# Moving the wide work of a step behind the wait for the maxima, in a single-core attention and feed-forward kernel

## The chip, the cores and the metric

The kernel runs on one core of one Trainium2 chip. The metric is device time in microseconds. Of the kernel before there are three runs: 6168.65, 6160.35 and 6164.67 us, median 6164.67. The engines are called PE (TensorE, matrix products, with PEld for its weight loads), DVE (VectorE), ACT (ScalarE), POOL (GpSimd) and SP (SyncE, which here issues the DMAs). PE's granted clock over the profiled execution was 0.986 of full speed.

## The reference

One layer of attention with relative positions, then a feed-forward layer with a router, each between layer norms and with a residual:

```python
def attn(x, ...):                      # x: (16, 1024, 256), 16 heads of 16
    q, k, v = (split_heads(lin(x, W, b)) for W, b in ((Wq, bq), (Wk, bk), (Wv, bv)))
    rel = rel_emb[r[None, :] - r[:, None] + 511]
    qk = einsum('bhld,bhrd->bhlr', q, k) / 4 + einsum('bhld,lrd->bhlr', q, rel)
    out = einsum('bhlr,bhrd->bhld', softmax(qk, axis=-1), v)
    return lin(merge_heads(out), Wo, bo)

def ffn(x, ...):                       # 6 experts of rank 16, the best 2 are used
    h = einsum('bsi,eri->bser', x, routed_A)
    routed = einsum('bseo,bse->bso', einsum('bser,eor->bseo', h, routed_B), sparse_w)
    return x @ base_W.T + base_b + (x @ shared_A.T) @ shared_B.T + routed

x = x + layernorm(attn(layernorm(x)))
x = x + layernorm(ffn(layernorm(x)))
```

## The kernel before

The 16 x 1024 rows are cut into 128 tiles t of 128 rows of queries. A tile is worked in 16 steps g = 0 to 15: `jp = g // 4` is the quarter of the keys (256 of them, in two blocks c = 0, 1), `k = g % 4` the block of 32 queries, of all 16 heads at once. The tiles overlap: while tile t goes through its scores, PE also makes the projections of a later tile n (`proj`), finishes the attention of the tile before (`a`) and does the feed-forward layer of the one before that (`b`). Tiles 2 to 127 have all parts and are the main loop, unrolled six times.

Each engine has its own queue, whose order is the order in which the code is written; semaphores tie the queues together. A step g on PE is, before the change:

1. `scores(g, 0)`: 8 matmuls (line 681) and 12 (line 687) into one PSUM bank of `sc`.
2. `transpose_max` (line 695): turns the row maxima `r1`, which DVE found in the scores of step g-1, into `p_max` in the PSUM bank `pm`.
3. `scores(g, 1)`: another 20 matmuls, then the signal `s_scores`.
4. `wide`: work into the PSUM bank `pw`. With k = 1 and k = 2 it is a half of the value product (`pv`, line 714), with k = 3 the transposition of the result (`transpose_parts`, line 721), with k = 0 and jp < 3 a projection of tile n (line 726 in step 0, line 735 in steps 4 and 8).
5. `mixed`: work into the bank `pm`, where DVE still reads `p_max`: a transposed row of `nm` with k = 1 (line 754), and in steps 0, 3, 8, 10, 11 and 12 transpositions and products of the `a` and `b` parts. Ahead of each stands `maxima_read`, the wait for `s_nmr`.
6. `shift` (line 704): 16 matmuls that subtract the maxima from the scores of step g-1, with `nmm` as weights. It waits for `s_nm`.

DVE does in each step: `spread` of g-1, that is `nm` (line 1000, a reduce that reads `p_max`, signal `s_nmr`) and then `nmm` (line 1003, a multiply, signal `s_nm`); the maximum of the scores of step g (line 991, called `r` in the profile); and `side`, small operations of the other parts. In step 5 `side` holds the router's `gate` (line 1034), `ceq` (line 1039) and `cgt` (line 1040), in step 6 three more operations on these, in step 14 the statistics of `x1` and `y2n`, in step 15 `xn1`. ACT copies what PE leaves in `pw` and `pm` (line 868) and takes the exponential of the shifted scores (line 876); it waits for each in the order of its own queue, in step 3 for `hf`, then `parts`, then the exponential. The scores have three buffers. POOL splits numbers into two halves of 16 bits and does additions; its chain `wp`, `osum`, `qkb`, `qkh`, `qkl` (lines 599 to 568) begins when ACT has copied the last `parts` of a tile, in step 3.

Of the kernel before, what the change touches and what calls it, by code (L numbers as in the profile page):

```python
# [20 lines left out]
NG = NJP * NI  # L21
# [17 lines left out]
def buffer(t, g):  # L39


    return (t * NG + g) % NBUF


def sandwich_kernel(nc, x, wqT, bq, wkT, bk, wvT, bv, woT, bo, relT, baseT, base_b,
# [13 lines left out]
    with ctx:  # L59
# [3 lines left out]
        def sem(name):  # L63
            return ctx.enter_context(nc.semaphore(name))
# [200 lines left out]
        s_nmr = sem("s_nmr")  # L265
# [13 lines left out]
        def batch_of(t):  # L279
            return t // TPB  # L280
# [387 lines left out]
        def _(pe):  # L668
# [39 lines left out]
            def pv(jp, half):  # L708

                for col in (2 * half, 2 * half + 1):  # L710
                    for c in range(2):
                        for q in range(4):
                            h = 4 * col + q
                            last = mm(pw[32 * q:32 * q + 32, col * P:(col + 1) * P], vs[:, 2 * jp + c, h, :],  # L714
                                      prob[:, jp % 2, c, h, :], start=(c == 0), stop=(c == 1))
                return last

            def transpose_parts(stage):
                pe.wait_ge(s_ot, stage + 1)
                for col in range(4):  # L720
                    last = nc.tensor.transpose(pw[:, col * P:(col + 1) * P], ot[:, col, :], ident[:, :])  # L721
                last.then_inc(s_ott, 1)

            def transpose2(dst, src):
                for c in range(2):
                    last = nc.tensor.transpose(dst[:, c * P:(c + 1) * P], src[:, c * P:(c + 1) * P],
                                               ident[:, :])
                return last

            def product(dst, *pairs):  # L730


                steps = [(lhs(i), rhs(j)) for lhs, rhs in pairs for i, j in ((0, 0), (0, 1), (1, 0))]
                for m, (lhs, rhs) in enumerate(steps):
                    last = mm(dst, lhs, rhs, start=(m == 0), stop=(m == len(steps) - 1))  # L735
                return last

            def both(lhs, rhs, cols=slice(None)):

                return [(lambda i, c=c: lhs[:, i, c, cols], lambda j, c=c: rhs[:, j, c, :]) for c in range(2)]  # L740

            def maxima_read(t, g, old):

                if old:
                    pe.wait_ge(s_nmr, t * NG + g)

            def mixed(t, g, att, a, b):


                jp, k = divmod(g, NI)  # L750
                old = a if g == 0 else att
                if k == 1 and (a if jp == 0 else att):
                    maxima_read(t, g, old)
                    mm(p_n[:, 0:H], nm[:, (jp - 1) % 2, :], ident16[:, 0:H], start=True, stop=True)\  # L754
                        .then_inc(s_nmtp, 1)
                    return s_nmt, t * NJP + jp
                if g == 0 and b:
                    maxima_read(t, g, old)
                    pe.wait_ge(s_xn1, t - 1)
                    transpose2(p_t, xn1).then_inc(s_x1Tp, 1)  # L760
                    return s_x1T, t - 1
                if g == 3 and b:

                    maxima_read(t, g, old)
                    pe.wait_ge(s_x1T2, t - 1)
                    product(p_t[:, 0:NH], *both(x1T2, w_a2)).then_inc(s_hp, 1)
                    return s_hf, t - 1
                if g == 8 and a:
                    maxima_read(t, g, old)
                    pe.wait_ge(s_o, t)  # L770
                    transpose2(p_t, o[:, :, :].rearrange("p h d -> p (h d)")).then_inc(s_oTp, 1)
                    return s_oT, t
                if g == 11 and a:
                    maxima_read(t, g, old)
                    pe.wait_ge(s_oT2, t)
                    product(p_t, *both(oT2, w_o2)).then_inc(s_wo, 1)
                    return s_y0, t
                if g == 10 and b:
                    maxima_read(t, g, old)
                    pe.wait_ge(s_hw, t - 1)  # L780
                    nc.tensor.transpose(p_n[0:NA, :], hw[:, :], ident[:, :]).then_inc(s_hTp, 1)
                    return s_hT, t - 1
                if g == 12 and b:
                    maxima_read(t, g, old)
                    pe.wait_ge(s_hT2, t - 1)
                    product(p_t, *both(x1T2, w_base2), (lambda i: hT2[:, i, :], lambda j: w_b2[:, j, :]))\
                        .then_inc(s_y2p, 1)
                    return s_y20, t - 1
                return None

            def wide(t, n, g, att, proj, a):

                jp, k = divmod(g, NI)
                if k and (a if jp == 0 else att):
                    pj = (jp - 1) % NJP
                    if k == 1:
                        pe.wait_ge(s_exp, t * NG + g - 1)
                        pe.wait_ge(s_vs[pj], batch_of(t - 1 if jp == 0 else t) * 16 + 16)

                        if proj and jp < 3:  # L800
                            pe.wait_ge((s_xT, s_qkf, s_vf)[jp], n + 1)
                        else:
                            pe.wait_ge(s_part, t * NJP + jp - 1)
                        pv(pj, 0)
                    elif k == 2:
                        pv(pj, 1).then_inc(s_pv, 1)
                    else:
                        transpose_parts(t * NJP + jp - 1)
                if k == 0 and jp < 3 and proj:

                    if a if jp == 0 else att:
                        pe.wait_ge(s_part, t * NJP + jp - 1)
                    elif jp == 0:
                        pe.wait_ge(s_vf, n)
                    if jp == 0:
                        pe.wait_ge(s_xn, n + 1)
                        transpose2(pw[:, 0:2 * P], xn).then_inc(s_xTp, 1)
                    elif jp == 1:
                        pe.wait_ge(s_xT2, n + 1)
                        for m, w in enumerate((w_q2, w_k2)):  # L820
                            for e in range(2):
                                last = product(pw[:, (2 * m + e) * P:(2 * m + e + 1) * P],
                                               *both(w, xT2, slice(e * P, (e + 1) * P)))
                        last.then_inc(s_qkp, 1)
                    else:
                        pe.wait_ge(s_qkf, n + 1)
                        product(pw[:, 0:D], *both(xT2, w_v2)).then_inc(s_vp, 1)

            def tile(t, n, att, proj, a, b, ph=None):
                read = None  # L830
                for g in range(NG):
                    jp, k = divmod(g, NI)
                    old = a if g == 0 else att
                    if att:
                        if k == 0:
                            pe.wait_ge(s_tw[jp], t * 16 + 16)
                            pe.wait_ge(s_ks[jp], batch_of(t) * 96 + 96)
                        if g == 0:
                            pe.wait_ge(s_qm, t * 96 + 96)
                        if jp == 0:  # L840
                            pe.wait_ge(s_mask, t * NI + k + 1)
                        free = t * NG + g - NBUF + 1
                        if not (isinstance(free, int) and free <= 0):
                            pe.wait_ge(s_exp, free)
                        scores(g, 0, buffer(ph, g), ph % 2)
                    if read is not None:
                        pe.wait_ge(*read)
                    if old:
                        transpose_max(t * NG + g)
                    if att:  # L850
                        scores(g, 1, buffer(ph, g), ph % 2).then_inc(s_scores, 1)

                    wide(t, n, g, att, proj, a)
                    read = mixed(t, g, att, a, b)
                    if old:
                        shift(buffer(ph, g - 1), t * NG + g)

            passes(pe, tile)


# [277 lines left out]
```

## Time and profile before

| what | value |
|---|---|
| runs | 6168.65, 6160.35, 6164.67 us |
| profiled execution | 6168.65 us |
| its span, first to last instruction | 6166.9 us |
| PE busy | 5870.1 us, 161792 matmuls |
| DVE busy | 4998.3 us, 81% |
| POOL, ACT busy | 3349.6 us (54%), 3069.7 us (50%) |
| DMA | 589.60 MB, mean 96 GB/s |

The busy share of an engine is an average; what the engine waits for is read from the list of waits and from the timeline, where instructions of one line that follow each other are merged into one row (so 32 records of line 714 are one row of 1.08 us). The start of a row is when the first of them began. Matmuls overlap in the pipeline, so a row of PE can begin before the one ahead of it has ended. All rows of timelines below are of one tile of the main loop, near the middle of the execution: step 2 begins near 2987.5 us, step 6 near 2998.8, step 12 near 3016.5.

### The profile page before, as it was taken

What the parts mean: (1) busy time and instruction counts of PE and PEld (TensorE: products, weight loads), DVE (VectorE), ACT (ScalarE), POOL (GpSimd) and SP (SyncE); (2) the same over time, 40 slices, a digit from 0 to 9 for tenths busy, and PEclk for the clock granted to TensorE, in tenths of its full rate; (3) what the DMA queues carried; (4) which work ended last, traced back from release to release, by engine and by line L of the source; (5) the groups of instructions that cost most, each with busy time, mean ns of one, the idle gap of its engine ahead of it and who ended that gap; (6) DMA issues with size and microseconds to landing.
All of it is one profiled execution on the core that took longest, in us unless ns stands there. A gap on an engine that the chain in (4) does not pass through costs nothing.

```text
span 6166.9 us, 379525 instructions
## 1 busy us (share of the span) xinstructions
PE 5870.1 (95%) x161792; PEld 5396.8 (88%) x161792; DVE 4998.3 (81%) x10289; ACT 3069.7 (50%) x5145; POOL 3349.6 (54%) x5226
## 2 busy tenths in 40 slices
PE   3999999999999999999999999999999999999997
PEld 2998988889898888988898988888898989898896
DVE  2788888888888888888888888888888878888886
ACT  1555555555455555545555555555555545555553
POOL 4455555555555555555555555555555555555555
PEclk7999999999999999999999999999999999999998
DMA  4334343343433334343343433434333343433432
GB/s 109 94 83 108 93 107 89 90 108 87 108 92 98 95 90 107 87 106 94 83 112 91 105 88 92 106 86 112 89 98 96 93 103 84 108 95 84 114 89 51
DMA packets 1461396, 589.60 MB, mean 96 GB/s; under 512 B 1127504, under 2 KB 1425472, under 8 KB 1459696
## 3 DMA queue, kind: packets, MB, share of 16 engines
q1 hardware_dynamic: 1459696, 565.02, 36.4%
q8 instruction: 1301, 21.32, 1.5%
q14 instruction: 399, 3.27, 0.2%
HBM read 476.43 MB, written 89.78 MB: 92 GB/s over the span
## 4 chain that ended last, share of the span: by engine, by line
PE 72%; DVE 14%; issue 6%; DVEq 5%; POOLq 1%; ACT 1%; POOL 1%; SPq 0%; DMA 0%
PE sc L687 18%; PE pw L714 13%; PE sc L704 13%; PE sc L681 12%; DVE r L991 6%; PE pm L735 4%; PE pw L735 4%; DVEq L1002 4%; PE pm L695 4%; PE pw L721 2%; DVE nmm L1003 2%; DVE xn L957 2%; DVE nm L1000 1%; DVE gate L1034 1%; DVE y2n L957 1%
## 5 line engine op out<-in xcount | busy, mean ns | idle before, releaser
L991 DVE TRANSPOSE_TENSOR_REDUCE r<-sc 128x32 f16<-128x1024 f32 x2048 | 2543.9, 1242 | 46.0 <-PE sc L687 45.1
L876 ACT ACTIVATE prob<-sc 128x1024 f32<-128x1024 f32 x2048 | 2097.9, 1024 | 294.4 <-PE sc L704 265.6
L687 PE MATMUL sc<-rm,tw 128*128 128x48 f16 (+1 forms) x49152 | 2148.5, 195 | 7.8 <-issue 7.3
L687 PEld LDWEIGHTS sc<-rm,tw 128*128 128x128 f16 x49152 | 1757.2, 100 | 9.5 <-issue 8.7
L681 PE MATMUL sc<-qm,ks 96*128 96x64 f16 x32768 | 1639.6, 193 | 52.5 <-DMA ks<-qk_s 28.3
L704 PE MATMUL sc<-nmm,pick 128*128 128x64 f16 x32768 | 1299.0, 193 | 95.6 <-DVE nmm L1003 84.5
L704 PEld LDWEIGHTS sc<-nmm,pick 128*128 128x128 f16 x32768 | 1128.1, 98 | 264.9 <-DVE nmm L1003 193.5
L681 PEld LDWEIGHTS sc<-qm,ks 96*128 96x128 f16 x32768 | 1300.4, 98 | 67.9 <-issue 50.4
L1000 DVE TENSOR_REDUCE nm<-pm 16x32 f16<-16x256 f32 x2048 | 836.3, 408 | 562.8 <-PE pm L695 549.4
L714 PE MATMUL pw<-prob,vs 128*32 128x128 f32 x32768 | 1114.3, 276 | 13.0 <-issue 4.3
L553 POOL TENSOR_TENSOR rm<-raw,mask_r 128x192 f16<-128x192 f16 (+1 forms) x1545 | 886.1, 602 | 34.6 <-DMA raw<-qk_s 23.2
L714 PEld LDWEIGHTS pw<-prob,vs 128*32 128x32 f32 x32768 | 840.4, 110 | 73.7 <-issue 17.5
L1003 DVE TENSOR_TENSOR nmm<-nm,mask_h 16x64 f16<-16x64 f16 x2048 | 590.1, 288 | 204.6 <-issue 19.4
L695 PE MATMUL pm<-ident,r 128*128 128x128 f16 x4096 | 571.7, 221 | 0.9 <-DVE r L991 0.8
L566 POOL TENSOR_TENSOR oT<-oT,one 128x256 f16<-128x256 f32 x128 | 78.4, 612 | 866.9 <-ACT oT L868 866.9
L868 ACT ACTIVATE ot<-pw 128x512 f32<-128x512 f32 x512 | 304.9, 595 | 486.3 <-PE pw L714 486.3
L868 ACT ACTIVATE nmt<-pm 128x16 f32<-128x16 f32 x512 | 93.7, 183 | 766.3 <-PE pm L754 766.3
L599 POOL TENSOR_TENSOR wp<-parts,wst 128x1088 f32<-128x1088 f32 x128 | 262.4, 2050 | 184.7 <-ACT parts L868 184.7
L560 POOL TENSOR_TENSOR ve<-mv,eps 128x1 f32<-128x1 f32 x521 | 113.6, 218 | 411.7 <-DVE mv L954 411.5
L562 POOL TENSOR_TENSOR rs<-ve,mhalf 128x1 f32<-128x1 f32 x521 | 288.2, 553 | 76.4 <-issue 2.5
L721 PE MATMUL pw<-ident,ot 128*128 128x128 f32 x2048 | 325.0, 281 | 0.7 <-ACT ot L868 0.7
L566 POOL TENSOR_TENSOR hT<-hT,one 112x128 f16<-112x128 f32 x128 | 51.1, 399 | 487.2 <-ACT hT L868 487.2
(129 smaller groups left out, 5958.9 us busy)
## 6 DMA issues: line engine op xcount, KB each, us to landing
raw<-qk_s SPq DMA_DIRECT2D x3096, 64.0 KB, 2.7
tw<-tw_s SPq DMA_DIRECT2D x512, 288.0 KB, 3.6
v_s<-vpad SPq DMA_DIRECT2D x136, 256.0 KB, 3.4
vs<-v_s SPq DMA_DIRECT2D x64, 512.0 KB, 4.4
qm<-qk_s SPq DMA_DIRECT2D x774, 32.0 KB, 2.1
ks<-qk_s SPq DMA_DIRECT2D x384, 64.0 KB, 3.3
xin<-x SPq DMA_DIRECT2D x138, 128.0 KB, 3.4
qk_s<-qkh SPq DMA_DIRECT2D x272, 64.0 KB, 2.9
```

The costliest lines, as they stand in the source:

```text
L553: last = g.tensor_tensor(rm[:, i, :, c * H:(c + n) * H].rearrange("p m (h e) -> p m h e", e=n), src[:, :, :, q:q + n], mask_r[:, c:c + n]. ...
L681: last = mm(bank[:, 2 * h * IW:(2 * h + 2) * IW], ks[:, h, j:j + P], qm[:, qb, 2 * h:2 * h + 2, i * IW:(i + 1) * IW], start=(h == 0), stop ...
L687: last = mm(out3[:, :, OCT * m + q:OCT * m + q + n], tw[:, s, jp, u:u + P], rm[:, i, m, r * H:(r + n) * H].rearrange("p (h e) -> p h e", e=n),
L695: last = mm(p_max[:, c * P:(c + 1) * P], r1[:, c * H:c * H + P], ident16[:, :], start=True, stop=True)
L704: last = mm(pairs[:, :, h, :], pick[:, h, :], nmm[:, :, :], start=False, stop=True, skip_group_check=True)
L714: last = mm(pw[32 * q:32 * q + 32, col * P:(col + 1) * P], vs[:, 2 * jp + c, h, :], prob[:, jp % 2, c, h, :], start=(c == 0), stop=(c == 1))
L721: last = nc.tensor.transpose(pw[:, col * P:(col + 1) * P], ot[:, col, :], ident[:, :])
L735: last = mm(dst, lhs, rhs, start=(m == 0), stop=(m == len(steps) - 1))
L876: A(prob[:, jp % 2, :, :, i * IW:(i + 1) * IW], sc[:, 2 * buf:2 * buf + 2, :].rearrange("p c (h i) -> p c h i", i=IW), ACT.Exp).then_inc(s ...
L991: v.tensor_reduce(r1[:, 0:2 * H], sc[:, 2 * buf:2 * buf + 2, :].rearrange("p c (h i) -> p (c h) i", i=IW), axis=AX.X, op=ALU.max, apply_tr ...
L1000: v.tensor_reduce(part, p_max[0:H, :].rearrange("h (q i) -> h i q", i=IW), axis=AX.X, op=ALU.max, negate=True).then_inc(s_nmr, 1)
L1003: v.tensor_tensor(nmm[0:H, :, :], part.rearrange("h (a i) -> h a i", a=1) .to_broadcast((H, 2, IW)), mask_h[:, :, :], ALU.mult).then_inc(s ...
```

## The change

On PE alone, `maxima_read` is gone. Each step that has a shift now waits for `s_nmr` once, directly ahead of `mixed`, also in the steps where `mixed` does nothing. `wide` stays ahead of this wait where k = 1 and in steps 0 and 8; in all others it comes behind it and behind `mixed`.

```diff
-            def maxima_read(t, g, old):
-
-                if old:
-                    pe.wait_ge(s_nmr, t * NG + g)
-
             def mixed(t, g, att, a, b):
 
 
                 jp, k = divmod(g, NI)
-                old = a if g == 0 else att
                 if k == 1 and (a if jp == 0 else att):
-                    maxima_read(t, g, old)
+
                     mm(p_n[:, 0:H], nm[:, (jp - 1) % 2, :], ident16[:, 0:H], start=True, stop=True)\
                         .then_inc(s_nmtp, 1)
                     return s_nmt, t * NJP + jp
                 if g == 0 and b:
-                    maxima_read(t, g, old)
                     pe.wait_ge(s_xn1, t - 1)
...
@@ -850,8 +838,14 @@
                     if att:
                         scores(g, 1, buffer(ph, g), ph % 2).then_inc(s_scores, 1)
 
-                    wide(t, n, g, att, proj, a)
+                    wide_first = k == 1 or g in (0, 8)
+                    if wide_first:
+                        wide(t, n, g, att, proj, a)
+                    if old:
+                        pe.wait_ge(s_nmr, t * NG + g)
                     read = mixed(t, g, att, a, b)
+                    if not wide_first:
+                        wide(t, n, g, att, proj, a)
                     if old:
                         shift(buffer(ph, g - 1), t * NG + g)
```

PE's queue in step 6, from the last score matmul to the next step's first ones, before:

```order
L687 MATMUL sc<-rm,tw 128x16x3
L714 MATMUL pw<-prob,vs 32x128 x16
L704 MATMUL sc<-nmm,pick 128x2x32 [waits s_nm]
L704 MATMUL sc<-nmm,pick 128x2x32 x15
L681 MATMUL sc<-qm,ks 128x64 [waits s_exp]
L681 MATMUL sc<-qm,ks 128x64 x7
```

and after the change:

```order
L687 MATMUL sc<-rm,tw 128x16x3
L714 MATMUL pw<-prob,vs 32x128 [waits s_nmr]
L714 MATMUL pw<-prob,vs 32x128 x15
L704 MATMUL sc<-nmm,pick 128x2x32 [waits s_nm]
L704 MATMUL sc<-nmm,pick 128x2x32 x15
L681 MATMUL sc<-qm,ks 128x64 [waits s_exp]
L681 MATMUL sc<-qm,ks 128x64 x7
```

The value product (line 714) now carries the wait for `s_nmr`, and the shift (line 704) stands behind it as before. Steps 2 and 14 are the same, step 7 has line 721 and step 4 line 735 in its place.

PE's queue in step 3, where `mixed` is the product of `x1T2` and `w_a2` (line 735) and `wide` the transposition of `ot` (line 721), before:

```order
L687 MATMUL sc<-rm,tw 128x16x3
L721 MATMUL pw<-ident,ot 128x128 [waits s_ot]
L721 MATMUL pw<-ident,ot 128x128 x3
L735 MATMUL pm<-w_a,x1T 128x118 [waits s_x1T2,s_nmr]
L735 MATMUL pm<-w_a,x1T 128x118 x5
L704 MATMUL sc<-nmm,pick 128x2x32 [waits s_nm]
L704 MATMUL sc<-nmm,pick 128x2x32 x15
```

and after:

```order
L687 MATMUL sc<-rm,tw 128x16x3
L735 MATMUL pm<-w_a,x1T 128x118 [waits s_x1T2,s_nmr]
L735 MATMUL pm<-w_a,x1T 128x118 x5
L721 MATMUL pw<-ident,ot 128x128 [waits s_ot]
L721 MATMUL pw<-ident,ot 128x128 x3
L704 MATMUL sc<-nmm,pick 128x2x32 [waits s_nm]
L704 MATMUL sc<-nmm,pick 128x2x32 x15
```

The two have changed places, and the wait for `s_nmr` is now ahead of both. Step 11 is alike, with `w_o2` and `oT2`.

PE's queue in step 10, where `mixed` is the transposition of `hw` (line 781 before, 770 after), before:

```order
L687 MATMUL sc<-rm,tw 128x16x3
L714 MATMUL pw<-prob,vs 32x128 x16
L781 MATMUL pm<-ident,hw 112x128 [waits s_hw,s_nmr]
L704 MATMUL sc<-nmm,pick 128x2x32 [waits s_nm]
L704 MATMUL sc<-nmm,pick 128x2x32 x15
```

and after:

```order
L687 MATMUL sc<-rm,tw 128x16x3
L770 MATMUL pm<-ident,hw 112x128 [waits s_hw,s_nmr]
L714 MATMUL pw<-prob,vs 32x128 x16
L704 MATMUL sc<-nmm,pick 128x2x32 [waits s_nm]
L704 MATMUL sc<-nmm,pick 128x2x32 x15
```

The transposition and its two waits went ahead of the value product. No matmul was added or removed, and the queues of DVE, ACT, POOL and SP are the same in both kernels.

## Rows read from the trace of the kernel before

**Rows 1.** Busy time of the engines, and the page's chain that ended last, by engine.

```profile
PE 5870.1 (95%) x161792; PEld 5396.8 (88%) x161792; DVE 4998.3 (81%) x10289; ACT 3069.7 (50%) x5145; POOL 3349.6 (54%) x5226
...
PE 72%; DVE 14%; issue 6%; DVEq 5%; POOLq 1%; ACT 1%; POOL 1%; SPq 0%; DMA 0%
```

**Rows 2.** List of waits: engine, line, waited for; us in total, times, longest us.

```profile
DVE nm L1000 <- PE pm L695: 549.4, 926, 4.4
...
PE sc L704 <- DVE nmm L1003: 84.5, 234, 1.1
```

**Rows 3.** Timeline of PE, steps 6 and 7: start us, us, engine, line.

```profile
3000.14 1.08 PE L714 MATMUL pw<-prob,vs 128*32 128x128 f32 x32
3001.72 0.64 PE L704 MATMUL sc<-nmm,pick 128*128 128x64 f16 x16 [0.51 <-DVE nmm L1003]
...
3003.27 0.52 PE L687 MATMUL sc<-rm,tw 128*128 128x48 f16 x12
3003.62 0.63 PE L721 MATMUL pw<-ident,ot 128*128 128x128 f32 x4
3004.33 0.64 PE L704 MATMUL sc<-nmm,pick 128*128 128x64 f16 x16
```

**Rows 4.** Timeline of DVE, steps 5 to 7.

```profile
2999.20 0.53 DVE L1034 TENSOR_SCALAR gate<-eg,rg 128x6 f32<-128x6 f32 x1
...
2999.91 1.15 DVE L1040 TENSOR_TENSOR cgt<-gate 128x36 f32<-128x36 f32 x1
3000.99 0.41 DVE L1000 TENSOR_REDUCE nm<-pm 16x32 f16<-16x256 f32 x1
...
3003.60 0.40 DVE L1000 TENSOR_REDUCE nm<-pm 16x32 f16<-16x256 f32 x1
```

**Rows 5.** Groups by form, DVE: count, busy us, mean ns of one, idle before.

```profile
L1040 DVE TENSOR_TENSOR cgt<-gate 128x36 f32<-128x36 f32 x128 | 147.4, 1151 | 0.0
...
L1043 DVE TENSOR_TENSOR ceqt<-ceq,tri 128x36 f32<-128x36 f32 x128 | 25.1, 196 | 11.8
```

**Rows 6.** Timeline of all engines, step 12.

```profile
3017.43 0.41 DVE L1000 TENSOR_REDUCE nm<-pm 16x32 f16<-16x256 f32 x1 [1.03 <-PE pm L695]
...
3017.46 0.52 PE L687 MATMUL sc<-rm,tw 128*128 128x48 f16 x12
...
3017.90 0.83 PE L735 MATMUL pm<-w_base,x1T 128*128 128x256 f16 x6
```

**Rows 7.** Timeline of PE, steps 2 and 3.

```profile
2988.15 0.52 PE L687 MATMUL sc<-rm,tw 128*128 128x48 f16 x12
2988.60 1.08 PE L714 MATMUL pw<-prob,vs 128*32 128x128 f32 x32
2989.61 0.64 PE L704 MATMUL sc<-nmm,pick 128*128 128x64 f16 x16
...
2991.03 0.52 PE L687 MATMUL sc<-rm,tw 128*128 128x48 f16 x12
2991.39 0.63 PE L721 MATMUL pw<-ident,ot 128*128 128x128 f32 x4
2991.86 0.48 PE L735 MATMUL pm<-w_a,x1T 128*128 128x118 f16 x6
```

**Rows 8.** Timeline of POOL, steps 5 and 6.

```profile
2998.66 1.04 POOL L566 TENSOR_TENSOR qkh<-qkb,one 128x512 f16<-128x512 f32 x1 [0.20 <-issue]
2999.84 1.17 POOL L568 TENSOR_TENSOR qkl<-qkb,qkh 128x512 f16<-128x512 f32 x1
```

**Rows 9.** Timeline of all engines, step 10.

```profile
3011.95 0.41 DVE L1000 TENSOR_REDUCE nm<-pm 16x32 f16<-16x256 f32 x1
...
3012.00 1.08 PE L714 MATMUL pw<-prob,vs 128*32 128x128 f32 x32
```

**Rows 10.** Timeline of all engines, step 15.

```profile
3026.22 0.41 DVE L1000 TENSOR_REDUCE nm<-pm 16x32 f16<-16x256 f32 x1
...
3026.45 0.64 PE L721 MATMUL pw<-ident,ot 128*128 128x128 f32 x4
```

More of the change, by code:

```diff
@@ L762, in mixed @@
                 if g == 3 and b:
-                    maxima_read(t, g, old)
                     pe.wait_ge(s_x1T2, t - 1)
@@ L768, in mixed @@
                 if g == 8 and a:
-                    maxima_read(t, g, old)
                     pe.wait_ge(s_o, t)
@@ L773, in mixed @@
                 if g == 11 and a:
-                    maxima_read(t, g, old)
                     pe.wait_ge(s_oT2, t)
@@ L778, in mixed @@
                 if g == 10 and b:
-                    maxima_read(t, g, old)
                     pe.wait_ge(s_hw, t - 1)
@@ L783, in mixed @@
                 if g == 12 and b:
-                    maxima_read(t, g, old)
                     pe.wait_ge(s_hT2, t - 1)
```

## The prediction

> **What bounds the kernel now.** Three views, from coarse to fine. The page's busy times and its chain of waits come first: PE is busy 95% of the span and holds 72% of the chain that ended last, DVE 81% and 14% [rows 1]. So PE sets the pace, and what is to be found is where PE stands still. The list of waits answers that: of PE's waits inside the main loop, the largest is the shift (line 704) waiting for `nmm` from line 1003, 84.5 us in 234 places [rows 2]. The third view is the timeline of one tile, read step by step: one tile is 16 steps g = 0 to 15, and tiles t = 2 to 127, 126 of them, run all parts. I read the tile that begins near 2983 us.
>
> In step 6 PE starts the second half of the value product at 3000.14, 32 records that last 1.08 us, and then stands 0.51 us before the shift at 3001.72 [rows 3]. DVE is the reason: its `cgt` lasts 1.15 us, so `nm` starts only at 3000.99 and ends at 3001.40, and `nmm` follows it [rows 4]. 126 x 0.51 = 64 us, three quarters of the 84.5 us. That this repeats in each tile is in the table by form: `cgt` has a mean of 1151 ns over 128, a sister of the same shape (`ceqt`) one of 196 ns [rows 5].
>
> **What the change does to one step.** PE's queue is in order. A step ends with the shift, which needs `nmm`, made from `nm`. Before, "wide" work (value product, transposition of its result, projections) stands ahead of the wait for `nm` and so covers DVE's reduce as well as its multiply. After, in steps 2, 3, 4, 6, 7, 10, 11, 14 and 15, the wait for `nm` (semaphore s_nmr) stands in front of the wide work, which covers only the multiply. No matmul is added or removed. In one step alone the new order can never be earlier: wide work starts at the later of two moments where it started at the first alone. The price of a step is the end of `nm`, plus the signal, less the moment at which PE was free, and PE is given back whatever it had waited for `nmm` afterwards. The signal is measured where the wait already stands directly behind the scores, in step 12: `nm` ends at 3017.84, the product starts at 3017.90, so 0.06 us; the last score matmuls started at 3017.46, so a step that DVE follows at once starts its next work 0.44 after them [rows 6]. Queued behind each new wait is all later PE work, with ACT's exponential and DVE's next maximum behind that.
>
> Steps 3, 4 and 11 (unhindered, `nm` follows PE). In step 3 line 721 starts at 2991.39, 0.36 after the scores' last group at 2991.03 [rows 7]; steps 4 and 11 show the same distance. With 0.44 in place of 0.36 each loses 0.08. The order of lines 721 and 735 turns round in 3 and 11, with the same matmuls; I take 0 for it. The turned pair is not in the trace; the old one follows at 0.47 [rows 7], and it could hardly gain or lose more than a third of that, 0.16. Step 4's two projections still hide `nmm` as before. Sum 3 x 0.08 = 0.24.
>
> Steps 2 and 14: the value product starts 0.45 after the scores' last group (2988.60 against 2988.15 [rows 7]), later than the 0.44 of the signal. Cost 0; bounds 0 and 0.1 each.
>
> Step 6: the wait ends at 3001.40 + 0.06 = 3001.46, where the product started at 3000.14 before. Product to shift, unhindered, takes 1.01 (2988.60 to 2989.61 [rows 7]). The shift moves to 3002.47 from 3001.72: +0.75. `nm` here does not depend on the new waits but on `cgt`, which ends at 3001.06, 0.05 after POOL's `qkl` at 3001.01 [rows 4, 8]. That POOL chain begins with `wp`, behind ACT's copy of `parts` in step 3, which the turned order puts a little later; 0.05 more. Bounds 0.55 (POOL's chain keeps its old time while PE comes 0.24 later) and 1.0. I take 0.80.
>
> Step 7: before, line 721 started at 3003.62 and the shift at 3004.33, 1.06 after the scores' last group (3003.27), held by the `nmm` behind an `nm` that ends at 3004.00 [rows 3, 4]. DVE was late because of its three operations after `cgt`. PE now comes 0.8 later and DVE only as much later as its own operations require, so `nm` again follows PE: start at 0.44, plus 0.47 for the transposes, shift at 0.91 instead of 1.06. This gives back 0.15. Steps 8 and 9 keep their order and cost nothing.
>
> Step 10: the transpose of `hw` goes ahead of the value product. `nm` ended at 3012.36 where PE was ready at 3012.00 [rows 9], but PE is then 0.7 later and most of this is gone; the pause between product and next load moves rather than vanishes. 0.05, bounds -0.1 and 0.42.
>
> Step 15: `nm` ends at 3026.63, signal 3026.69, against 3026.45 for line 721 [rows 10]: 0.24. Step 0 behind it waits for DVE's `xn` anyway, and PE's lateness is absorbed there; I take 0.05, bounds 0 and 0.24.
>
> **Sum.** Per tile 0.24 + 0 + 0.80 - 0.15 + 0.05 + 0.05 = 0.99 us; times 126 = 125 us. The profiled execution took 6168.65 us (span 6166.9), so 6293; it is 4.0 us above the median of the three runs, so 6289, or 6290 rounded. Nothing outside these steps changes: ACT gets `hf`, `hT` and `y0` earlier, but PE's next wait for them lies behind a full round of scores and shows no loss in the list before.
>
> **The rivals.**
> *Lateness adds up.* If DVE comes later by as much as PE does, every step pays its full distance: 0.24, then 1.32, 0.44 (3004.00 + 0.06 against 3003.62), 0.42 and 0.24 for steps 6, 7, 10 and 15, less the 0.51 already stood: 2.15 per tile, 271 us, 6436 on the median. For it: DVE's maximum follows `nmm`. Against: in step 7 DVE had been the later one, and `nm` waited for PE for 549.4 us in 926 places [rows 2].
> *DVE sets the pace and takes the delay up.* If what step 6 loses (0.65 with step 7) is regained before the tile ends, 0.34 stays: 43 us, 6208. For it: DVE's 81% share. Against: those same 926 places, where DVE idles for PE.
> *Faster: POOL slips out of `cgt`'s way.* `gate` starts at 2999.20 inside POOL's `qkh` (2998.66 to 2999.70) and `cgt` ends with `qkl` [rows 4, 8]. If POOL's chain came over 0.54 later against DVE, `gate` and `cgt` would run first, some 0.3 and 0.95 shorter. `nm` would then follow PE, and step 6 loses its wait of 0.51, step 7 its 0.15 and step 8 a few hundredths: -0.70, with +0.24, +0.10 and 0.05 at most for the rest, so -0.3 per tile, -39 us, 6126. Against: the chain's start moves by some 0.1, PE's and so DVE's by about as much. The point from which it decides is 0.54 us.
> The Trainium skill, SBUF, "Who interferes with whom", says that a VectorE instruction with two SBUF inputs and a GpSimd instruction that reads SBUF exclude each other, and that the one issued first goes first; by that rule the slip would indeed free `cgt`. Here the trace agrees as to the block (1151 against 196 ns), and no row shows the reverse order.
>
> **How the numbers follow.** Forecast 0.78, adding up 0.08, taken up 0.09 (its lower end, 0.02, within 0.2%), POOL slips 0.05. A change under 0.2%, 12 us, can't be told from none here. So faster 0.05, same 0.02, slower 0.93. The forecast's own ends: 0.70 per tile (step 6 at 0.55, the rest as taken) gives 6253; 1.5 per tile (steps 2 and 14 at 0.1, step 6 at 1.0, 10 and 15 at 0.15 each) 6350. The range goes a little into both neighbours: 6245 to 6365.
>
> **What would show it.** In the profile after: PE's line 714 waiting on `nm` (line 1000) in 126 places with about 1.3 us each; the list's wait of the shift on `nmm` shrunk from 84.5 to some 20 us; `cgt` still near 1.15 us; line 721 of step 7 about 0.44 behind its scores; a tile's length up by 1 us. Wrong would be: `cgt` near 0.2 us; idle of line 721 of over 0.2 us in each tile (adding up); or line 695 waiting less than before by as much as line 714 waits more.

## The result, and the profile after

The changed kernel took 6230.68 us (median of 4 runs, 6229.27 to 6231.38), the kernel before, with its runs on the same chip, 6163.78 us. The ratio is 1.011, with a 95% interval of 1.0098 to 1.0124: slower by 67 us, where 125 had been forecast, and below the range's lower end of 6245. The profiled execution took 6235.45 us, its span is 6233.7.

The page of the changed kernel, its row of busy times and its chain by engine, against [rows 1]:

```profile
PE 5857.5 (94%) x161792; PEld 5428.1 (87%) x161792; DVE 4998.5 (80%) x10289; ACT 3139.6 (50%) x5145; POOL 3362.3 (54%) x5226
...
PE 73%; DVE 13%; issue 6%; DVEq 6%; POOLq 1%; ACT 1%; POOL 0%; SPq 0%; DMA 0%
```

PE has the same 161792 matmuls and is busy 12.6 us less in a span that is 66.8 us longer. So the added time is idle time of PE. Its list of waits (us in total, times, longest us), against [rows 2]:

```profile
DVE nm L994 <- PE pm L695: 581.2, 1045, 2.0
...
PE pw L714 <- DVE nm L994: 132.8, 126, 1.1
...
PE sc L704 <- DVE nmm L997: 22.4, 103, 0.3
```

The wait of the shift on `nmm` fell from 84.5 to 22.4 us, as forecast. The new one, of the value product on `nm`, is there 126 times, 1.05 us each on PE. Together that is 70.7 us more. Steps 6 and 7 of one tile, on PE, against [rows 3]. The rows of line 695 are where `transpose_max` begins; from here on a step's length is the distance from its row of line 695 to the next one:

```profile
3079.83 0.28 PE L695 MATMUL pm<-ident,r 128*128 128x128 f16 x2
...
3080.18 0.52 PE L687 MATMUL sc<-rm,tw 128*128 128x48 f16 x12
3081.71 1.08 PE L714 MATMUL pw<-prob,vs 128*32 128x128 f32 x32 [1.02 <-DVE nm L994]
3082.73 0.64 PE L704 MATMUL sc<-nmm,pick 128*128 128x64 f16 x16
...
3083.44 0.52 PE L687 MATMUL sc<-rm,tw 128*128 128x48 f16 x12
3083.80 0.28 PE L695 MATMUL pm<-ident,r 128*128 128x128 f16 x2
...
3084.14 0.52 PE L687 MATMUL sc<-rm,tw 128*128 128x48 f16 x12
3084.58 0.66 PE L721 MATMUL pw<-ident,ot 128*128 128x128 f32 x4
3085.07 0.63 PE L704 MATMUL sc<-nmm,pick 128*128 128x64 f16 x16
...
3086.13 0.28 PE L695 MATMUL pm<-ident,r 128*128 128x128 f16 x2
```

Before, the value product of step 6 started 0.46 after the scores' last group and the shift waited; now the product starts at 3081.71, 1.53 after the scores' last group, and the shift 1.02 behind it. Step 6 is 3.97 us long and step 7 only 2.33. DVE in the same stretch, against [rows 4]:

```profile
3080.18 1.15 DVE L1034 TENSOR_TENSOR cgt<-gate 128x36 f32<-128x36 f32 x1
3081.26 0.41 DVE L994 TENSOR_REDUCE nm<-pm 16x32 f16<-16x256 f32 x1
...
3081.87 1.25 DVE L985 TRANSPOSE_TENSOR_REDUCE r<-sc 128x32 f16<-128x1024 f32 x1
...
3084.11 0.41 DVE L994 TENSOR_REDUCE nm<-pm 16x32 f16<-16x256 f32 x1 [0.16 <-PE pm L695]
```

`nm` of step 6 ends at 3081.67, and 0.04 later the product starts: the signal is as short as assumed. The rows of the kernel before that I had not read are those of line 695, of the same tile as [rows 3]:

```profile
2999.34 0.28 PE L695 MATMUL pm<-ident,r 128*128 128x128 f16 x2
...
3002.43 0.52 PE L687 MATMUL sc<-rm,tw 128*128 128x48 f16 x12
3002.91 0.28 PE L695 MATMUL pm<-ident,r 128*128 128x128 f16 x2
...
3005.51 0.28 PE L695 MATMUL pm<-ident,r 128*128 128x128 f16 x2
```

and the row of DVE's maximum that belongs to it:

```profile
3001.60 1.25 DVE L991 TRANSPOSE_TENSOR_REDUCE r<-sc 128x32 f16<-128x1024 f32 x1
```

In the changed kernel line 695 begins 0.36 after the group of line 687 ahead of it (3083.44 to 3083.80). In the kernel before it is 0.48 (3002.43 to 3002.91): the maximum ended at 3002.85, and line 695 started 0.06 later. So PE waited for DVE a second time at the end of step 6, by 0.12, and again at the end of steps 7 and 8: as means over 122 tiles line 695 came 0.14, 0.13 and 0.12 later than it does where DVE is ready. The list of waits does not name these waits; they are short, and PE's earlier matmuls still count as busy. In the kernel before, these two steps were 3.57 and 2.60 us long.

The two kernels step by step, as means of the distance between the first weight loads of line 695, over 122 tiles of the main loop of each trace (changed minus before, us per tile):

| step | measured | forecast | what it is |
|---|---|---|---|
| 3 | +0.05 | +0.08 | wait for `nm`, turned order |
| 4 | +0.13 | +0.08 | wait for `nm`, and in a few tiles a late `nm` (last section) |
| 6 | +0.43 | +0.80 | wait for `nm` ahead of the value product |
| 7 | -0.27 | -0.15 | DVE no longer late |
| 8 | -0.08 | 0 | the same |
| 10 | +0.20 | +0.05 | turned order, and a late `nm` in a third of the tiles |
| 11 | -0.01 | +0.08 | turned order |
| 15 and 0 | +0.07 | +0.05 | wait for `nm`, then `xn` |
| the rest | -0.01 | 0 | |
| sum | +0.52 | +0.99 | times 126: 65 us and 125 us |

### The profile page after: what moved, and what is told of

The parts are those of the page before. It is cut to its first block, busy times and chain, and to the rows that moved or that the text cites. A ratio compares the mean times of both kernels' runs of the same rounds, so it can differ in the third digit from the quotient of the medians.

```text
span 6233.7 us, 379790 instructions
## 1 busy us (share of the span) xinstructions
PE 5857.5 (94%) x161792; PEld 5428.1 (87%) x161792; DVE 4998.5 (80%) x10289; ACT 3139.6 (50%) x5145; POOL 3362.3 (54%) x5226
## 4 chain that ended last, share of the span: by engine, by line
PE 73%; DVE 13%; issue 6%; DVEq 6%; POOLq 1%; ACT 1%; POOL 0%; SPq 0%; DMA 0%
PE sc L687 18%; PE pw L714 14%; PE sc L704 13%; PE sc L681 12%; DVE r L985 5%; PE pm L735 5%; DVEq L996 4%; PE pw L735 4%; PE pm L695 3%; PE pw L721 3%; DVE xn L951 2%; DVE nm L994 1%; DVE nmm L997 1%; DVE y2n L951 1%; PE pm L748 1%
## 5 line engine op out<-in xcount | busy, mean ns | idle before, releaser
L704 PE MATMUL sc<-nmm,pick 128*128 128x64 f16 x32768 | 1299.1, 193 | 28.9 <-DVE nmm L997 22.4
L704 PEld LDWEIGHTS sc<-nmm,pick 128*128 128x128 f16 x32768 | 1146.1, 98 | 167.9 <-issue 104.5
L553 POOL TENSOR_TENSOR rm<-raw,mask_r 128x192 f16<-128x192 f16 (+1 forms) x1545 | 886.7, 603 | 33.9 <-DMA raw<-qk_s 22.4
L862 ACT ACTIVATE parts<-pw 128x272 f32<-128x272 f32 x512 | 203.5, 398 | 268.8 <-PE pw L721 262.1
```

The lines of the kernel that those rows point to most:

```text
L553: last = g.tensor_tensor(rm[:, i, :, c * H:(c + n) * H].rearrange("p m (h e) -> p m h e", e=n), src[:, :, :, q:q + n], mask_r[:, c:c + n]. ...
L704: last = mm(pairs[:, :, h, :], pick[:, h, :], nmm[:, :, :], start=False, stop=True, skip_group_check=True)
L862: return A(dst, src, ACT.Copy)
```

## The experiments

All kernels were timed in turn with the kernel before on their chip; a ratio is to that. Where I give a change in us it is the difference of the medians. Step lengths of experiments are means over 16 or 17 tiles in the middle of each trace, or over 122 tiles of the main loop where that is said.

### Step 6 alone

```diff
+                    if old and g == 6:
+                        pe.wait_ge(s_nmr, t * NG + g)
                     wide(t, n, g, att, proj, a)
                     read = mixed(t, g, att, a, b)
```

> The kernel before with one new wait: in step 6 alone PE waits for nm ahead of the value product. Theory A (DVE paces steps 6 to 8 and takes most of the delay up: behind nm of step 6 its maximum, its side work and the next nm follow without a gap, and PE waits for the maximum at line 695): from nm of step 6 to line 695 of step 9 the kernel before takes 7.26 us and the changed one 7.57, so +0.31 per tile, 39 us, about 6203. Theory B (PE paces, as I had predicted): +0.75 - 0.15 = 0.60 per tile, 76 us, about 6240.

Measured: 6190.40 us against 6161.44, ratio 1.0038 (1.0025 to 1.0052), +29 us. PE of steps 6 and 7:

```profile
3010.67 0.28 PE L695 MATMUL pm<-ident,r 128*128 128x128 f16 x2
...
3012.71 1.08 PE L714 MATMUL pw<-prob,vs 128*32 128x128 f32 x32 [1.18 <-DVE nm L1002]
...
3014.79 0.28 PE L695 MATMUL pm<-ident,r 128*128 128x128 f16 x2
...
3017.03 0.29 PE L695 MATMUL pm<-ident,r 128*128 128x128 f16 x2
```

Step 6 is 4.12 us (mean +0.58), step 7 only 2.24 (mean -0.34), together +0.24 per tile or 30 us. The shift moves by 0.73 (mean of 122 tiles), as I had thought; the step is longer by less than that, and more than half of it comes back in the next. Theory B (76 us) falls; theory A (39) was 10 us too high.

### All but step 6

```diff
-                    wide_first = k == 1 or g in (0, 8)
+                    wide_first = k == 1 or g in (0, 6, 8)
```

> The changed kernel with step 6 as before. Theory A: steps 6 to 8 lose only 0.09 per tile in the changed kernel, and without the wait step 6 would even be 0.17 shorter than before (POOL's chain comes earlier against PE), so 0.26 less per tile than the changed kernel: about 6198. Theory B: 0.65 less per tile, 82 us, about 6149.

Measured: 6198.88 us, ratio 1.0057 (1.0043 to 1.0070), +37 us, as theory A said. Step 6 alone (29) and all but step 6 (37) add up to 66, against 67 for the whole change. Step 6, whose code is here that of the kernel before, is 0.20 shorter than in it (122 tiles).

### Step 10 alone

```diff
-                    wide(t, n, g, att, proj, a)
+                    if g != 10:
+                        wide(t, n, g, att, proj, a)
                     read = mixed(t, g, att, a, b)
+                    if g == 10:
+                        wide(t, n, g, att, proj, a)
```

> The kernel before with the order of step 10 alone turned (transpose of hw with its waits, then the second half of the value product). Theory A (a switch between a product of 32 columns and other work costs a pause on each side, and the transpose no longer hides it): +0.20 per tile, 25 us, about 6189. As predicted (the pause only moves): +0.05 per tile, 6 us, about 6170.

Measured: 6180.78 us, ratio 1.0029 (1.0019 to 1.0040), +19 us; step 10 is 0.17 longer. The turned order in the changed kernel, PE of step 10, against [rows 9]:

```profile
3092.04 0.52 PE L687 MATMUL sc<-rm,tw 128*128 128x48 f16 x12
3092.47 0.32 PE L770 MATMUL pm<-ident,hw 128*112 128x128 f32 x1
3092.72 1.08 PE L714 MATMUL pw<-prob,vs 128*32 128x128 f32 x32
3093.74 0.64 PE L704 MATMUL sc<-nmm,pick 128*128 128x64 f16 x16
```

In this tile the transposition starts 0.43 after the scores' last group, where it waits for `nm`, the product 0.25 behind it and the shift 1.02 behind the product: 1.70 in all. In the old order it was 0.45 to the product, 1.01 to the transposition and 0.16 to the shift, 1.62. The product stands 0.25 behind the transposition where the shift stood 0.16 behind it, and the pause ahead of a product that follows the scores (0.45, where line 721 has 0.36) is no longer there to cover the wait. So turning the pair saves nothing and costs 0.08.

The rest of the 0.20 is in other tiles. Over 122 tiles of the changed kernel the shift moves by 0.08 in the 82 in which `nm` ends on time, and by 0.36 in the 40 in which it ends late (0.66 on average behind the scores' last group, in place of 0.38). The late ones are the last two of each six tiles of the unrolled loop, in which step 10 is 0.28 and 0.52 longer, and the tile that the prediction read is the last of its six. In such a last tile DVE pauses in step 9, in the kernel before as in the changed one:

```profile
3009.46 0.51 DVE L1003 TENSOR_TENSOR nmm<-nm,mask_h 16x64 f16<-16x64 f16 x1 [0.47 <-issue]
```

The profile names no releaser for this pause, and its cause stays open.

### `cgt` moved on DVE

```diff
                 if g == 5 and b:
...
                     v.tensor_tensor(ceq[:, :, :], gf, ge, ALU.is_equal)
-                    v.tensor_tensor(cgt[:, :, :], gf, ge, ALU.is_gt)
                 if g == 6 and b:
+                    v.tensor_tensor(cgt[:, :, :], gf, ge, ALU.is_gt)
                     dve.drain()
```

(`gf` and `ge` are formed again in step 6.) First on the kernel before:

> The kernel before with DVE's cgt moved from the end of step 5's side work to the start of step 6's, where POOL has ended qkl. Theory A (cgt was long only because it stood behind POOL's qkl; PE loses 0.51 us visibly and some 0.14 more at line 695 through it): cgt near 0.2 us, about -0.65 per tile, 82 us, about 6082. Theory C (only the visible wait goes): -0.51 per tile, about 6100. Theory D (POOL blocks it at the new place too, or DVE's total length sets steps 6 to 8): within 15 us of 6164.

Measured: 6090.81 us, ratio 0.9881 (0.9866 to 0.9896), 71 us faster than the kernel before, and so the fastest of all these kernels. It lies between theories A (6082) and C (6100): the shift of step 6 comes 0.53 earlier, and 0.08 more comes back at line 695, where A had 0.14. Theory D falls. The group of `cgt` (count, busy us, mean ns):

```profile
L1043 DVE TENSOR_TENSOR cgt<-gate 128x36 f32<-128x36 f32 x128 | 19.3, 151 | 0.0
```

It takes 151 ns in place of 1151 [rows 5]. Step 6 is 0.63 shorter, step 7 0.06 longer. Then the same move on the changed kernel:

> The changed kernel with DVE's cgt moved to the start of step 6's side work, to be compared with the kernel before with the same move (6091 us). Theory A (DVE is late in steps 6 to 8 whatever PE does): nm of step 6 then ends 0.63 after the scores' last loads, so its new wait costs about 0.2 and step 7 gives 0.1 back; with steps 3, 4, 10, 15 unchanged at +0.35: about +0.45 per tile, 57 us, 6148. Theory B (the wait in step 6 costs what nm is late there, nothing is given back): the 0.60 of my prediction falls to 0.2, so about +0.6 per tile in all, 76 us, 6167.

Measured: 6138.05 us, ratio 0.9964 (0.9951 to 0.9978), 47 us over the kernel before with the same move. That one ran on another chip; each against the kernel before on its own chip, it is 50 us (20 gained in place of 71). The change costs less where DVE is less late, but it still costs, in steps 3, 4 and 10. Theory A was 10 us too high, B 29.

### Step 7 alone

```diff
+                    if old and g == 7:
+                        pe.wait_ge(s_nmr, t * NG + g)
                     wide(t, n, g, att, proj, a)
```

> The kernel before with one new wait, in step 7 alone, ahead of line 721. PE comes to line 721 some 0.45 us later in each tile. Theory A: the shift moves by about 0.1 only, and PE then waits 0.14 less for DVE's maximum at line 695: 0 per tile, within 6 us of 6161. Theory E (lateness adds up): 0.44 per tile, 55 us, 6217. Theory F (only the shift's own move counts): 0.11 per tile, 14 us, 6175.

Measured: 6163.35 us against 6158.31, ratio 1.0008 (1.0000 to 1.0017), +5 us. Line 721 starts 0.43 later in each tile, step 7 is 0.08 longer, and step 8 is 0.08 shorter. A wait of 0.43 us on the busiest engine costs nearly nothing here: the sharpest blow to "lateness adds up".

### Who takes the delay up

If it is DVE's own lateness behind `nm` of step 6 that takes PE's delay up, taking that lateness away must make the wait dear. The base moves DVE's router work out of steps 6 and 7:

```diff
                     v.tensor_tensor(lg[:, :], hf[:, NA:NH], b_rt[:, :], ALU.add)
+                    v.tensor_copy(hw[:, 0:R], hf[:, 0:R])
...
-                if g == 6 and b:
-                    dve.drain()
-                    v.tensor_tensor(ceqt[:, :, :], ceq[:, :, :], tri[:, :, :], ALU.mult)
-                    dve.drain()
-                    v.tensor_tensor(cadd[:, :, :], cgt[:, :, :], ceqt[:, :, :], ALU.add)
-                    dve.drain()
-                    v.tensor_reduce(rank[:, :], cadd[:, :, :], axis=AX.X, op=ALU.add)
...
-                if g == 7 and b:
-
+                if g == 8 and b:
+                    dve.drain()
+                    v.tensor_tensor(ceqt[:, :, :], ceq[:, :, :], tri[:, :, :], ALU.mult)
+                    dve.drain()
+                    v.tensor_tensor(cadd[:, :, :], cgt[:, :, :], ceqt[:, :, :], ALU.add)
+                    dve.drain()
+                    v.tensor_reduce(rank[:, :], cadd[:, :, :], axis=AX.X, op=ALU.add)
                     dve.drain()
                     v.scalar_tensor_tensor(out=sw[:, :], in0=rank[:, :], scalar=2.0, in1=gate[:, :],
                                            op0=ALU.is_lt, op1=ALU.mult)
-                    v.tensor_copy(hw[:, 0:R], hf[:, 0:R])
-                if g == 8 and b:
```

> The kernel before with DVE's router work moved away from steps 6 and 7: ceqt, cadd, rank and sw to step 8's side work, the copy of hf to step 4's. The cgt that is blocked stays in step 5, so nm of step 6 is as late as before. It serves as the base of the next kernel. Theory A (DVE paces steps 6 to 8): step 7 gets shorter by 0.34 and step 8 by up to 0.2, step 9 or 10 gives some of it back: about -0.25 per tile, 6130. If DVE does not pace them: 6161.

Measured: 6177.02 us (11 runs, 6166.73 to 6191.67) against 6158.31, ratio 1.0031 (1.0022 to 1.0040): 19 us slower, where both theories had it faster or equal. The steps say why: step 7 is 0.35 and step 8 0.12 shorter, as theory A says, but step 9 is 0.59 longer, since `nm` there now comes behind six small operations of step 8. PE, steps 6 and 7:

```profile
3046.51 0.28 PE L695 MATMUL pm<-ident,r 128*128 128x128 f16 x2
...
3050.01 0.29 PE L695 MATMUL pm<-ident,r 128*128 128x128 f16 x2
...
3052.26 0.29 PE L695 MATMUL pm<-ident,r 128*128 128x128 f16 x2
```

As a base it does what it should: step 7 is at 2.25, PE's own length. On it, the wait of step 6:

> The kernel relieved of DVE's router work in steps 6 and 7, with the one new wait of step 6. Theory A: with DVE no longer late behind nm of step 6, nothing takes the delay up, and the wait costs about 0.6 us per tile, 76 us over its base, against 29 us over the kernel before. Theory G (the delay is given back by PE itself, since line 721 behind a wait is faster): the same 29 us over its base.

Measured: 6245.79 us against 6158.31, ratio 1.0138 (1.0122 to 1.0155). That is 69 us over its base, and its fastest run (6240.40) is still 49 us over the slowest of the base. PE and DVE of steps 6 and 7:

```profile
3033.95 0.28 PE L695 MATMUL pm<-ident,r 128*128 128x128 f16 x2
...
3036.06 1.08 PE L714 MATMUL pw<-prob,vs 128*32 128x128 f32 x32 [1.24 <-DVE nm L1002]
...
3038.14 0.28 PE L695 MATMUL pm<-ident,r 128*128 128x128 f16 x2
...
3040.39 0.28 PE L695 MATMUL pm<-ident,r 128*128 128x128 f16 x2
```

```profile
3036.22 1.25 DVE L993 TRANSPOSE_TENSOR_REDUCE r<-sc 128x32 f16<-128x1024 f32 x1
3038.46 0.41 DVE L1002 TENSOR_REDUCE nm<-pm 16x32 f16<-16x256 f32 x1 [0.99 <-PE pm L695]
```

Step 6 is 4.19 us where the base has 3.50 (means: 0.61 more), and step 7 stays at 2.25. DVE has ended its maximum at 3037.47 and waits for PE until 3038.46. The same wait, in the same step, costs 69 us here and 29 us where DVE is late behind it. Theory G falls, since line 721 stands behind a delayed shift in both.

### Step 3 alone, and a further move on DVE

```diff
-                    wide(t, n, g, att, proj, a)
+                    if g != 3:
+                        wide(t, n, g, att, proj, a)
+                    elif old:
+                        pe.wait_ge(s_nmr, t * NG + g)
                     read = mixed(t, g, att, a, b)
+                    if g == 3:
+                        wide(t, n, g, att, proj, a)
```

> The kernel before with step 3 alone changed: wait for nm, product of line 735, then line 721. As predicted: +0.08 per tile, 10 us, 6168. From the traces since: ACT's copy of parts, and with it POOL's chain, starts 0.11 us earlier in the tile, which lets cgt and nm of step 6 end up to 0.17 earlier against PE; step 3 itself +0.05, step 4 +0.01 (or +1.4 us in the few tiles where DVE's xn falls behind POOL's wp): together -0.1 to 0 per tile, 6146 to 6160.

Measured: 6173.00 us (12 runs, 6157.88 to 6188.10) against 6165.93, ratio 1.0010 (1.0000 to 1.0020). The +10 us of the first expectation lie within the interval, the second (12 us faster to equal) only touches its end. The trace shows what the second had too small. Over 122 tiles step 3 is at +0.10, step 4 at +0.13 and step 6 at -0.14. In 110 of the tiles step 3 loses 0.10 and step 6 gains 0.08, and little else moves. In the other 12 DVE's `xn` falls behind POOL's `wp` (last section): step 4 is 1.32 longer, step 6 0.70 and step 7 0.34 shorter.

The last run adds two moves on DVE to that of `cgt`:

```diff
                     v.tensor_tensor(lg[:, :], hf[:, NA:NH], b_rt[:, :], ALU.add)
+                    v.tensor_copy(hw[:, 0:R], hf[:, 0:R])
...
-                if g == 7 and b:
+                if g == 8 and b:
 
                     dve.drain()
                     v.scalar_tensor_tensor(out=sw[:, :], in0=rank[:, :], scalar=2.0, in1=gate[:, :],
                                            op0=ALU.is_lt, op1=ALU.mult)
-                    v.tensor_copy(hw[:, 0:R], hf[:, 0:R])
-                if g == 8 and b:
-
                     dve.drain()
```

> The kernel before with cgt in step 6 (as in the fourth run, 6091 us), the copy of hf into hw moved from step 7 to step 4 and sw from step 7 to step 8, both ahead of steps in which a value product covers DVE. If DVE paces step 8: nm of step 8 ends 0.25 earlier, step 8 is 0.1 shorter, 12 us, 6079. If moved work costs as much at the new places: 6091.

Measured: 6108.49 us against 6165.93, ratio 0.9907 (0.9893 to 0.9921), where the move of `cgt` alone had 0.9881. Step 8 is 0.11 shorter as expected, and step 9 is 0.15 longer. So the move of `cgt` alone stays the best version, though the ends of the two intervals touch.

## Why the prediction was wrong

The direction was right, and so was how the new wait delays PE: no step can gain by it alone, and step 6 is where `nm` is late. What was wrong is how much of the delay PE is given back. The sum was nearly twice too large, 0.99 us per tile against 0.52, and the steps that failed are these. (Numbers without a source are means over 122 tiles.)

**Step 6, "+0.75", then "0.80".** The 0.75 was right: with step 6 alone the shift moves by 0.73. What I left out stands at the end of the step. Before, PE lost another 0.14 at line 695, waiting for DVE's maximum, and this is given back as well: the step is 0.59 longer, not 0.73. And the 0.05 for POOL's chain had the wrong sign. With line 735 ahead of 721, ACT's copy of `hf` is out of the way of its copy of `parts`, which now starts 0.11 earlier in the tile, while PE loses 0.17 in steps 3 to 5; so `nm` of step 6 ends 0.16 earlier against PE. The lower bound of 0.55 had this case in it. 0.59 less 0.16 is 0.43, what the changed kernel shows.

**Step 7, "gives back 0.15", and "steps 8 and 9 cost nothing".** For the shift of step 7 the 0.15 was right: it stands 0.93 behind the scores' last group in place of 1.06, where I had 0.91. But behind it line 695 waited for DVE's maximum again, by 0.13, and in step 8 by 0.09 more than now. Both are given back, so step 7 is 0.27 shorter and step 8 0.08. The term that I had put at nothing, PE's wait for DVE's maximum at line 695, is worth 0.14 + 0.13 + 0.09 = 0.36 us per tile in steps 6 to 8. My last sign of being wrong, that line 695 would wait less, came true in this part, against 1.05 us that line 714 waits more.

**The rival "DVE sets the pace and takes the delay up".** I gave it 0.09 because DVE waits for PE in 926 places. But there are 2048 steps. In the kernel before, `nm` waits for PE in steps 1, 3, 4 and 11 to 14 of at least 101 of 122 tiles, and in steps 5 to 9 of none. In [rows 4] and the row above, `nm`, `nmm`, the maximum, three small operations and the next `nm` follow each other from 3000.99 to 3004.00 without a wait. A count over the tile hid a stretch with another pacemaker. The pair of relieved kernels shows it: the same wait costs 69 us without DVE's work there, 29 with it. The rival as I wrote it, at 43 us, took too much back: step 6 is not made good in full, since DVE catches up as soon as PE is late enough (it waits 0.16 in step 7 of the changed kernel).

**Step 10, "0.05".** It is 0.20. I had argued that the pause only moves, and that PE's lateness would eat the wait. The turned pair costs 0.08 in every tile. And in a third of the tiles `nm` is late behind DVE's own work and pause in step 9, and being later on PE does not shorten that; so it is still late, and the wait adds about 0.3 there.

**Right:** steps 2 and 14 at nothing (0.00 and +0.03), steps 15 and 0 at 0.05 (0.07), the signal of 0.06, the fall of the shift's wait to about 20 us, and `cgt` near 1.15 us (1115 ns). "Line 714 with about 1.3 us each" came out at 1.05 on PE. Steps 3, 4 and 11 at 0.24 in all came out at 0.17, which is partly luck: 0.05 of step 4 comes from the blocked `xn` below, and in step 11 line 721 had on average already started 0.04 later than in the tile that I read.

**The sums.** The ends of the forecast were added up wrongly. With step 6 at 0.55 and the rest as taken the lower one is 0.74 per tile, 6258 us, not 0.70 and 6253; the upper one is 1.59, 6365 us, not 1.5 and 6350. The range would have begun higher still.

**The other rivals.** *Lateness adds up* fell most clearly with step 7 alone, +5 us for 0.43 us of waiting per tile. *POOL slips out of `cgt`'s way* did not happen: POOL's chain came earlier against DVE, not later. DVE's groups of `cgt` and `gate` in the changed kernel:

```profile
L1034 DVE TENSOR_TENSOR cgt<-gate 128x36 f32<-128x36 f32 x128 | 142.7, 1115 | 0.0
...
L1028 DVE TENSOR_SCALAR gate<-eg,rg 128x6 f32<-128x6 f32 x128 | 49.0, 382 | 9.9
```

`gate` is at 382 ns in place of 506, since POOL's `qkh` ends earlier against it; `cgt` is still blocked in all but 5 of 128 tiles, and in those it is free because it comes behind `qkl`. The run in which it was moved by hand shows what the slip would have brought, 71 us on the kernel before.

What stays open is the share of step 3: its run moved the time by 7 us with an interval that begins at nothing.

## What to carry to other kernels

On an in-order queue, work between two waits covers only what the second waits for; moving it behind the first gives up the cover of the longer part. But the price is not the sum of the new waits: look at each stretch for whether the other engine runs without a gap there, because in such a stretch a delay of this one is free until the other has caught up. And before moving work on the engine that waits, look at why the other is late: the 71 us here were in one DVE operation that had been placed beside a POOL operation.

## What the runs showed of the hardware

A DVE operation can be held up by a POOL operation for nearly all of the latter's length, and which one is held depends on a few hundredths of a microsecond. In step 3 POOL's `wp` starts close to DVE's `xn`. A usual tile of the changed kernel:

```profile
3073.04 0.37 DVE L951 TENSOR_SCALAR xn<-xin,mv,rs 128x256 f32<-128x256 f32 x1
3073.17 2.14 POOL L599 TENSOR_TENSOR wp<-parts,wst 128x1088 f32<-128x1088 f32 x1 [1.40 <-ACT parts L862]
```

In 5 of 128 tiles it goes the other way. All engines, steps 3 to 6 of such a tile:

```profile
3166.55 2.25 DVE L951 TENSOR_SCALAR xn<-xin,mv,rs 128x256 f32<-128x256 f32 x1
3166.61 2.04 POOL L599 TENSOR_TENSOR wp<-parts,wst 128x1088 f32<-128x1088 f32 x1 [1.39 <-ACT parts L862]
...
3168.72 0.40 DVE L994 TENSOR_REDUCE nm<-pm 16x32 f16<-16x256 f32 x1
...
3169.18 0.84 PE L735 MATMUL pw<-xT,w_q 128*128 128x128 f16 x12 [1.32 <-DVE nm L994]
...
3173.83 1.16 POOL L568 TENSOR_TENSOR qkl<-qkb,qkh 128x512 f16<-128x512 f32 x1
...
3175.21 0.19 DVE L1034 TENSOR_TENSOR cgt<-gate 128x36 f32<-128x36 f32 x1
```

`xn` took 2.25 us in place of 0.37 and `nm` of step 4 came 1.4 us late. It is the turned order of step 3 that brings this about, by starting `wp` earlier: `wp` begins 0.22 us behind `xn` in the kernel before, where no tile of the main loop shows it, and 0.12 behind it in the changed one. In the traces of all twelve kernels `xn` is short wherever its row begins 0.08 or more ahead of `wp`'s, and long wherever it is 0.06 or less. The wait of step 4 adds little: such a tile has step 4 longer by 1.49 in the changed kernel and by 1.32 with step 3 alone turned, where step 4 has its old order. About half is given back two steps later. DVE and PE are then so late that `cgt` finds `qkl` ended (0.19 us at 3175.21), and step 6 is 0.77 shorter than in the other tiles of the changed kernel. With step 6 restored this happened in 14 tiles (18.5 us of PE's waiting). It is what step 4 cost beyond 0.08.

By the rule of the Trainium skill (SBUF — State Buffer, "Who interferes with whom") `tensor_scalar` can enter a mode that takes the port pair shared with GpSimd, and the one that issues first keeps the other out for a whole instruction. The trace agrees as to the block: `xn` ends 0.15 us after `wp`, which took 2.04. As to the order it can't decide, since the blocked `xn` has a row that begins 0.06 ahead of `wp`'s.
